# Value products of the second batch in three float32r products, with operands split on GpSimd

## What is computed

```python
v = _split_heads(context @ v_w.T + v_b)          # (2, 4096, 256) @ (256, 256)
scores = jnp.einsum('bhqd,bhkd->bhqk', q, k) / jnp.sqrt(jnp.float32(HD))
scores = jnp.where(mask, -jnp.inf, scores)
ctx = jnp.einsum('bhqk,bhkd->bhqd', jax.nn.softmax(scores, axis=-1), v)
```

## Time and profile before

| | |
|---|---|
| runs of the kernel, median (lowest to highest) | 2047.43 us (2045.57 to 2051.0) |
| profiled execution, its own time | 2048.77 us |
| span from first to last instruction | 2047.4 us |
| mean granted TensorE clock | 0.959 |
| busy: PE, DVE, ACT, POOL | 1884.8, 1366.1, 1253.0, 625.7 us |

### The profile page before, as it was taken

How to read it: one execution, slowest core, us unless ns; L and a number is a source line. 1 busy time by engine, 2 the same in 40 slices (tenths; PEclk the granted TensorE clock), 3 DMA queues, 4 the chain that set the end, 5 groups by cost and what they waited for, 6 DMA issues and landing times.

```text
span 2047.4 us, 37473 instructions
## 1 busy us (share of the span) xinstructions
PE 1884.8 (92%) x13875; PEld 1202.5 (59%) x13875; DVE 1366.1 (67%) x3210; ACT 1253.0 (61%) x2818; POOL 625.7 (31%) x737
## 2 busy tenths in 40 slices
PE   7999999998998899999999788899988799789998
PEld 4555555554575455555555457789456788555656
DVE  4776678884767577667788376654276997577382
ACT  3787778896444278777889462376264786265251
POOL 2211011112630211111110274585051565355151
PEclk9999999998998789999999898999999899899999
DMA  9677667760112857667763204153202341200110
GB/s 212 154 148 138 122 117 162 147 125 27 42 42 41 139 106 150 129 115 147 153 110 47 85 1 142 42 174 104 67 2 75 92 124 52 88 1 9 42 55 11
DMA packets 114356, 191.52 MB, mean 94 GB/s; under 512 B 17224, under 2 KB 67200, under 8 KB 107648
## 3 DMA queue, kind: packets, MB, share of 16 engines
q1 hardware_dynamic: 113184, 188.11, 41.7%
q10 hardware_dynamic: 992, 1.02, 0.2%
HBM read 135.20 MB, written 2.69 MB: 67 GB/s over the span
## 4 chain that ended last, share of the span: by engine, by line
PE 66%; DVE 22%; ACT 7%; issue 2%; DMA 1%; POOL 1%; SPq 0%; DVEq 0%; ACTq 0%; POOLq 0%
DVE WK L860 9%; PE PS L797 8%; PE PS L687 8%; PE PS L704 6%; PE PS L358 5%; PE PS L366 5%; PE PS L675 4%; PE PS L716 4%; PE PS L464 3%; PE PS L2394 2%; PE PS L491 2%; PE PS L2336 2%; PE PS L512 2%; ACT WK L563 2%; PE PS L1277 1%
## 5 line engine op out<-in xcount | busy, mean ns | idle before, releaser
L860 DVE TENSOR_REDUCE WK<-PS 128x1 f32<-128x1024 f32 x512 | 621.6, 1223 | 226.6 <-PE PS L687 172.2
L968 ACT ACTIVATE WK<-PS 128x512 f32<-128x512 f32 x840 | 464.5, 601 | 39.0 <-PE PS L687 25.0
L687 PEld LDWEIGHTS PS<-QSR,KSR 51*128 51x128 f32 x2048 | 251.4, 187 | 244.1 <-ACT WK L968 90.2
L687 PE MATMUL PS<-QSR,KSR 51*128 51x256 f32 x2048 | 379.6, 307 | 9.6 <-ACT WK L968 1.3
L675 PE MATMUL PS<-KSR,QSR 51*128 51x512 f32 x1024 | 371.5, 454 | 8.5 <-DMA QSR<-scratch_q 3.4
L797 PE MATMUL PS<-WK 128*32 128x256 f32 x2528 | 219.5, 394 | 0.6 <-ACT WK L952 0.5
L991 POOL TENSOR_TENSOR WK<-WK 128x512 fp32r<-128x512 f32 x62 | 79.3, 1278 | 442.5 <-ACT WK L929 231.9
L675 PEld LDWEIGHTS PS<-KSR,QSR 51*128 51x128 f32 x1024 | 186.3, 188 | 20.6 <-issue 12.5
L563 ACT ACTIVATE WK<-PS,WK 128x256 f32<-128x256 f32 (+1 forms) x320 | 140.6, 451 | 79.6 <-DVE WK L531 50.5
L593 POOL TENSOR_TENSOR WK<-WK 128x512 f32<-128x512 f32 x96 | 99.9, 1040 | 69.4 <-DVE WK L546 51.3
L1044 POOL TENSOR_SCALAR nbw<-WK 128x4 fp32r<-128x4 f32 x64 | 12.6, 197 | 353.1 <-DVE WK L866 345.9
(11 more groups left out here) (371 smaller groups left out, 3768.6 us busy)
## 6 DMA issues: line engine op xcount, KB each, us to landing
KSR<-WK SPq DMA_DIRECT2D x381, 128.0 KB
WB<-in_ctxT SPq DMA_DIRECT2D x78, 512.0 KB, 5.1
WK<-in_ctxT SPq DMA_DIRECT2D x40, 512.0 KB, 4.4
WK<-in_ctx SPq DMA_DIRECT2D x32, 512.0 KB, 3.9
WA<-in_ctxT SPq DMA_DIRECT2D x26, 512.0 KB, 5.2
QSR<-scratch_q SPq DMA_DIRECT2D x48, 128.0 KB, 4.2
WB<-in_L3f_qkv SPq DMA_DIRECT2D x2, 1536.0 KB, 6.2
WB<-in_L3f_w SPq DMA_DIRECT2D x2, 1536.0 KB, 9.6
```

The lines of the kernel that those rows point to most:

```text
L687: return pe.e.matmul(tile["S", L, s, i][:, j * 256:j * 256 + 256], KS[s % 4][HALF[i % 2], kt * 128:(kt + 1) * 128], QS[HALF[i % 2], g % 2, ...
L860: dv.e.tensor_reduce(mt[:, n:n + 1], tile["R", L, s, n].rearrange("p a b -> p (a b)"), AX, ALU.max).then_inc(*dv.at("R", L, s, n))
L968: ac.e.activation(PR[n % NPR], tile["S", L, s, i], ACT.Exp).then_inc(*ac.at("E", L, s, i))
```

## The change

The eight V of batch 1 in each of the two attentions are computed from split operands. The weights are split once, at step 6 ("WS"). At u == 0 of each step 8 to 15 ("VS") GpSimd rounds the whole context chunk (128 by 1024 elements) to float32r (`CTH`) and subtracts, which gives the low part (`CTL`); there is one such pair of buffers. At u == 2 TensorE waits for GpSimd ("cl") and issues 24 float32r products (high by high, high by low, low by high, for 4 row tiles and 2 halves of the contraction) in place of the 8 float32 ones. The V of batch 0 stay as they were.

```diff
+            if u == 0 and s == 6:
+                yield ("WS",)
+            if u == 0 and 8 <= s < 16:
+                yield "VS", s
...
+        VWH = sb("VWH", [128, 512], FR)
+        WBR = nc.alloc_sbuf_tensor_at("WBR", [128, 512], FR, offset=nc.sbuf_base - 4 * 8704)
...
+        CTH, CTL = WAR[:, 2048:3072], WAR[:, 3072:4096]
+        XWL = [WAR[:, 1024:1536], WBR[:, 0:512]]
...
+            def values_split(L, b):
+
+                wh, wl = (view(w, 0, 512, 2, 256) for w in (VWH, XWL[L]))
+                high, low = (view(x, 0, 1024, 2, 512) for x in (CTH, CTL))
+                for t in range(4):
+                    m = slice(t * 128, (t + 1) * 128)
+                    y = b.ap[:, t // 2, t % 2 * 256:t % 2 * 256 + 256]
+                    for k in range(2):
+                        pe.e.matmul(y, high[:, k, m], wh[:, k, :], start=k == 0, stop=False)
+                        pe.e.matmul(y, high[:, k, m], wl[:, k, :], start=False, stop=False)
+                        x = pe.e.matmul(y, low[:, k, m], wh[:, k, :], start=False, stop=k == 1)
+                return x
...
+                    if s is not None:
+                        pe.wait_ge(po, "cl", L, c)
+                        values_split(L, b).then_inc(*pe.at("V", L, bb, c))
+                        continue
...
+        def split_weight(L):
+
+            raw = XW[L]["v"].rearrange("p a b -> p (a b)")
+            po.wait_ge(pe, "V", L, 0, 7)
+            po.e.tensor_scalar(VWH[:, :], raw, 1.0, 1.0, ALU.mult, ALU.mult).then_inc(*po.at())
+            po.wait_ge(po)
+            po.e.tensor_tensor(XWL[L], raw, VWH[:, :].bitcast(F), ALU.subtract).then_inc(*po.at())
+
+        def split_context(L, s):
+
+            ct, sem, event = chunk(L, s - 8, s)
+            raw = ct.rearrange("p a b -> p (a b)")
+            po.wait_ge(sem, *event)
+            if s > 8:
+                po.wait_ge(pe, "V", L, 1, s - 9)
+            elif L == 0:
+                po.wait_ge(dv, "msk")
+            po.e.tensor_scalar(CTH, raw, 1.0, 1.0, ALU.mult, ALU.mult).then_inc(*po.at())
+            po.wait_ge(po)
+            po.e.tensor_tensor(CTL, raw, CTH.bitcast(F), ALU.subtract).then_inc(*po.at("cl", L, s - 8))
...
+                elif o[0] == "WS":
+                    split_weight(L)
+                elif o[0] == "VS":
+                    split_context(L, o[1])
```

## The result

The changed kernel is slower: 2111.94 us in the median of six runs (2099.76 to 2116.2) against 2048.53 us for the kernel before, a ratio of 1.0299 with an interval of [1.0275, 1.0323], some 61 us. The forecast was 2103 with a range of 2074 to 2126.

A forecast was written before the change was run, and what follows sets the result against it. TensorE, 92% busy and 66% of the chain, was taken as the bound. A net 31.7 us from V's delay plus 23.8 us of half clock made 55.5 on 2047.4: 2102.9, about 2103 us, range 2074 to 2126.

The forecast's parts named there:

- The place in the queue: GpSimd's chunk split queues behind the key split: each V starts 2.75 us later, net 31.7 us over 16 V.
- The upper bound of 1.78 for the rounding: GpSimd's slow rounding of the chunk, 1.78 us for 1.12: 10.6 us more over 16 V, 10% chance.
- V's length: On TensorE, 24 float32r products at 0.120 us take 2.88 us a V, against 3.65 before.
- the possible gain: The shorter V on TensorE saves 0.77 us each, 12.3 us for 16 V, at most.
- The clock: On TensorE, 14 of 16 stalls bring half clock, losing 1.7 us each: 23.8 us in all.
- the short form: After a stall, TensorE's half clock lasts 3.4 us, of which half, 1.7 us, is lost.
- The steady clock: Rival: TensorE's clock holds through the stalls, so only 31.7 us are added, 2079 us; 20%.
- The hidden split: Rival: GpSimd has both parts ready before V, each V saves 0.77 us, 2035 us; 4%.
- The small parts: Weights' split, row-maximum instructions and chunk DMA cost nothing; without idle GpSimd time the weights' split would cost 4 us.

The follow-up runs named there:

- e1_ahead: Changed kernel with the chunk split moved to u == 4 of the step before, ahead of the key split: 2034.54 us, ratio 0.9957 to the kernel before.
- after_again: The changed kernel itself, unaltered, measured again beside e4_again on one chip: 2107.44 us, ratio 1.0277 to the kernel before.
- e4_filler: Changed kernel with 22 float32r products on constant operands put before TensorE's wait for GpSimd: 2076.81 us, ratio 1.0166 to the kernel before.
- e4_again: The kernel of e4_filler measured again, beside after_again on one chip: 2077.21 us, ratio 1.0140 to the kernel before.
- e6_early: As e1_ahead, but the chunk split at u == 2 of the step before, ahead of the row maximum's instructions: 2101.77 us, ratio 1.0294 to the kernel before.

## Why the prediction was right

Direction, mechanism and size hold. Point by point:

- **The place in the queue.** V was forecast to start 3.75 us after the key split's end. It starts 231.11 - (226.23 + 1.29) = 3.59 us after it. The rounding takes 1.05 us (1.12 taken), the subtraction 2.34 (2.40). The other differences are small: V's release took 0.15 us for 0.07, and the rounding's record starts 0.04 before the key split's ends, where a gap of 0.08 was taken. The upper bound of 1.78 for the rounding, scaled from the L1680 median of the earlier trace rows, plays no part.
- **V's length.** 2.88 us forecast, 3.05 measured in e1_ahead (3.03 in a clean step of the changed kernel): the pace was right, the 0.1 us at either edge was left out. This term was mis-sized by 16 x 0.17 = 2.7 us, and it is what the possible gain lacks: 0.60 a step in e1_ahead for 0.77. By luck the 0.16 us that the split was quicker offset it in the changed kernel, so the clean step came out at 18.18 us for 16.21 + 1.98 = 18.19.
- **The clock.** 14 stalls at 1.7 us, 23.8 us, were forecast. The first profile has 13 of 16 V steps longer than the clean 18.0 to 18.2, and they hold 55.6 - 30.3 = 25.3 us above it (30.3 is eight times 18.18 less 16.21 and eight times 17.99 less 16.17). That the profiled total of 55.6 meets the forecast's 55.5 is luck in part: the clock's share came out 1.5 us above the forecast and the rest, 30.3 for 31.7, 1.4 below. Within the clock's share the short kind lost 1.5 us a step and not 1.7, and the long kind, to which the forecast gave no stall, 2.4. The step that failed in part is "Behind each stall V follows, dense work, so I take the short form": in six of the 16 the clock fell before V began, in after_again's profile in nine. There the V steps grew by 60.1 us, of which 60.1 - 30.3 = 29.8 are the clock's. The median, 2112 for 2103, has a lower mean clock than the profiled run, which fits more steps of the long kind, but of the six runs only the fastest has a profile, so this is argued and not shown. Against the kernel before run beside it, after_again came out 57.9 us slower.
- **The Trainium skill's rule** (TensorE: Matmul & The Clock Gate, HAM oscillation — how this bites in real kernels), that each return from a wait is paid again at the slow clock, holds here for 13 of 16 stalls in this profile and 14 of 16 in after_again's. The page's kernel waits for DMA, some 3 to 5 us each time; here the waits for GpSimd are 2.5 to 2.7 us. In e4_filler the same wait filled with products was not paid for.
- **The rivals.** The steady clock was put at 31.7 us above the kernel before; e4_filler, which makes it steady, is above it by 34 us by its ratio, and e4_again by 29. The hidden split was put at 12.3 us below; e1_ahead, which hides it, is 8.8 below. That its 2034.5 us meets the forecast's 2035 is luck, as the kernel before was 3.4 us faster beside it (2044.0 for 2047.4); the 3.5 us that the gain lacks are mostly V's mis-sized length. The small parts (weights' split, DMA, row maximum) cost nothing where they are, and e6_early shows that the row maximum is paid for when it loses its place.

## What to carry to other kernels

Work that is given to an engine with 7 us of idle time is free only if its place in that engine's queue is inside the idle time: look up what stands ahead of it, when that can start, and who waits for what stands behind. The same two instructions at three places of one list made the kernel 61 us slower, 60 us slower or 9 us faster than before. A stall of some 3 us on TensorE, once a step, cost nearly as much again in half clock; products that nobody needs, issued ahead of the wait, gave that part back, and the right place gave back all.

## What the hardware showed beyond the forecast

- The V steps with half clock come in two lengths, 19.5 to 19.7 us at a mean clock of 0.91 and 20.5 to 20.6 at 0.83, against 18.0 to 18.2 at 1.00. In attention 1 of the changed kernel the long kind follows itself, from 899.83 to 1002.17 five times 20.47 us. The two lengths go with where the clock falls: after V's start, for some 3.4 us, or during the wait before it, for some 6.8 us. No step of the 32 in the two profiles has another length of half clock. What decides between the kinds, and what makes the long one repeat, was not tried.
- A burst of 24 float32r products behind other work or behind a wait has 0.19 to 0.22 us between its first and second start, and 0.21 between its last and the next product's, for a pace of 0.119. At half clock the pace is 0.213 and the whole V takes 5.39 us (929.47 to 934.86).
- GpSimd's rounding to float32r of 128 by 1024 took 1.047 to 1.062 us in all sixteen, where the same instruction, 768 wide, had taken 0.831 to 1.798 us in another stage.
